# Expert stage of a two-layer gated block: new addresses for the tiles of normalized tokens and gated activations

## The reference

```python
x = x + tanh(g_xattn[0]) * L0_xattn(layernorm(x), ctx, ctx, ...)      # retention over four heads
x = x + tanh(g_ffn[0])   * L0_ffn(layernorm(x), w1, w2, gamma)        # ternary weights, 512 -> 2048 -> 512
x = x + tanh(g_xattn[1]) * L1_xattn(ctx, ctx, layernorm(x), ssm_kernel, D, 8)
x = x + tanh(g_ffn[1])   * L1_ffn(layernorm(x), Wg, bg, Wgate, ...)   # experts
```

```python
gate = xf @ Wg + bg                                  # 8 logits, the 6 highest are kept
w = softmax(kept)[:, :6] * routed_mask
g = einsum('td,ndh->tnh', xf, Wgate) + bgate
u = einsum('td,ndh->tnh', xf, Wup) + bup
eo = einsum('tnh,nhd->tnd', silu(g) * u, Wdown) + bdown
share = silu(xf @ Ws_up + bs_up) @ Ws_down + bs_down
out = einsum('tnd,tn->td', eo, w) + share
```

## Time and profile before

| what | value |
|---|---|
| median of three runs | 2049.53 us (2049.35 to 2049.96) |
| span of the profiled execution | 2045.1 us |
| outside the span, against that median | 4.4 us |
| PE busy | 1937.3 us, 95% |
| PEld busy | 1565.1 us, 77% |
| DVE busy | 1480.1 us, 72% |
| ACT, POOL busy | 1029.0 us, 1037.1 us |
| granted clock of TensorE, mean | 0.977 |

### The profile page before, as it was taken

The page is one execution under the profiler, slowest core; times in us unless marked ns, Lnnn a source line. Parts: engine busy times, 40 slices in busy tenths (PEclk is TensorE's granted clock), DMA queues, the critical chain, the costliest instruction groups (busy, mean ns, idle before and its releaser), DMA issues.

```text
span 2045.1 us, 27663 instructions
## 1 busy us (share of the span) xinstructions
PE 1937.3 (95%) x10020; PEld 1565.1 (77%) x10050; DVE 1480.1 (72%) x2229; ACT 1029.0 (50%) x1468; POOL 1037.1 (51%) x788
## 2 busy tenths in 40 slices
PE   6999779999996769999999999999999999999998
PEld 6888656666653658888888888888888888888786
DVE  6777579888884867867876876876886787687422
ACT  4457457767774354345336337336435633633532
POOL 1110154444430945765655665656566566666454
PEclk9999889999998879999999999999999999999999
DMA  6776325655664213324234233242242423422422
GB/s 221 291 247 241 150 62 142 165 163 139 140 131 116 73 31 124 106 70 139 76 105 145 78 114 129 77 120 97 95 124 68 140 80 100 148 75 72 133 90 67
DMA packets 170115, 249.72 MB, mean 122 GB/s; under 512 B 91356, under 2 KB 92764, under 8 KB 163708
## 3 DMA queue, kind: packets, MB, share of 16 engines
q1 hardware_dynamic: 169692, 247.86, 39.7%
q10 hardware_dynamic: 288, 0.10, 0.0%
HBM read 193.13 MB, written 33.69 MB: 111 GB/s over the span
## 4 chain that ended last, share of the span: by engine, by line
PE 64%; POOL 2%; issue 1%; DVE 1%; DVEq 0%; ACT 0%; POOLq 0%; ACTq 0%
PE e_ps_out L54 6%; PE e_ps_out L55 6%; PE e_ps_out L56 6%; PE e_ps_u L54 6%; PE e_ps_u L56 6%; PE e_ps_u L55 6%; PE e_ps_g L54 4%; PE e_ps_g L56 4%; PE e_ps_g L55 4%; PE e_ps_m L55 4%; PE e_ps_m L56 4%; PE e_ps_m L54 4%; PE e_ps_m L2873 1%; PE e_ps_m L2827 1%; PE e_ps_m L2863 1%
## 5 line engine op out<-in xcount | busy, mean ns | idle before, releaser
L1418 POOL TENSOR_TENSOR e_gu_lo<-e_gu_raw,e_gu_hi 128x1024 fp32r<-128x1024 f32 (+1 forms) x128 | 289.3, 2263 | 183.4 <-ACT e_gu_hi L1722 183.4
L2277 DVE TENSOR_REDUCE e_x3T<-e_zp 128x128 f32<-128x1024 f32 x124 | 258.4, 2084 | 6.5 <-ACT x_held L1837 5.3
L1423 POOL TENSOR_TENSOR e_dn_lo<-e_dn_raw,e_dn_hi 128x512 fp32r<-128x512 f32 x128 | 180.6, 1414 | 112.6 <-ACT e_dn_hi L1728 111.8
L54 PE MATMUL e_ps_u<-e_xn_hi,e_gu_hi 128*128 128x512 f32 x512 | 205.2, 401 | 0.0
L54 PE MATMUL e_ps_out<-e_hd_hi,e_dn_hi 128*128 128x512 f32 x512 | 204.0, 399 | 0.0
L56 PE MATMUL e_ps_u<-e_xn_hi,e_gu_lo 128*128 128x512 f32 x512 | 202.1, 395 | 0.0
L55 PE MATMUL e_ps_out<-e_hd_lo,e_dn_hi 128*128 128x512 f32 x512 | 202.0, 394 | 0.0
L55 PE MATMUL e_ps_u<-e_xn_lo,e_gu_hi 128*128 128x512 f32 x512 | 201.9, 394 | 0.0
L56 PE MATMUL e_ps_out<-e_hd_hi,e_dn_lo 128*128 128x512 f32 x512 | 201.9, 394 | 0.0
L2209 DVE TENSOR_TENSOR e_hd_lo<-gate_held,e_hd_hi 128x512 fp32r<-128x512 f32 x128 | 147.4, 1152 | 67.9 <-ACT e_hd_hi L1752 67.7
L1430 POOL TENSOR_TENSOR gate_held<-e_sg,e_wb 128x512 f32<-128x512 f32 x96 | 137.4, 1432 | 113.0 <-ACT e_sg L1736 71.7
(11 more groups left out here) (316 smaller groups left out, 5059.8 us busy)
## 6 DMA issues: line engine op xcount, KB each, us to landing
e_gu_raw<-in_mgu SPq DMA_DIRECT2D x96, 512.0 KB, 3.8
e_dn_raw<-in_md SPq DMA_DIRECT2D x128, 256.0 KB, 2.8
e_wb<-wts SPq DMA_DIRECT2D x8, 1536.0 KB, 7.4
c<-in_ctxT SPq DMA_DIRECT2D x8, 1024.0 KB, 7.0
raw_w<-in_w1T SPq DMA_DIRECT2D x8, 1024.0 KB, 5.0
x_held<-in_w2T SPq DMA_DIRECT2D x8, 1024.0 KB, 7.4
gates<-gate_held SPq DMA_DIRECT2D x8, 1024.0 KB, 5.5
vals<-o SPq DMA_DIRECT2D x8, 1024.0 KB, 5.2
```

The source lines that it names most:

```text
L54: nc.tensor.matmul(out, w_hi, x_hi, start=first, stop=False, skip_group_check=skip)
L1418: nc.gpsimd.tensor_tensor(gu_lo[:, s % 2, a], gu_raw[:, s % 2, a], f32(gu_hi[:, s % 2, a]), ALU.subtract).then_inc(gulo_done, 1)
L1423: nc.gpsimd.tensor_tensor(dn_lo[:, s % 2], dn_raw[:, s % 2], f32(dn_hi[:, s % 2]), ALU.subtract).then_inc(dnlo_done, 1)
L2277: nc.vector.tensor_reduce(x3T[:, lb].rearrange("p (b n) -> p b n", b=B)[:, :, hh * CD:(hh + 1) * CD], zv(5, (1, 8), (21, 8)), AX.X, ALU.ad ...
```

## The change

The tile `skip` is allocated behind all other tiles of the expert stage instead of in their middle. Two tiles that nothing writes or reads are added: `gap_xn`, 16 floats (64 bytes) in each partition, ahead of `xn_hi`, and `gap_hd`, 64 floats (256 bytes), ahead of `hd_hi`. No instruction changes but for its addresses.

```diff
     zp = sb("zp", [P, B, ZW])
-    skip = sb("skip", [P, NCH * CHD])
     x3T = sb("x3T", [P, KT, CH])
 
     xnat = sb("xnat", [P, TJ, D])
+    gap_xn = sb("gap_xn", [P, 16])
     xn_hi, xn_lo = sb("xn_hi", [P, KT, CH], F32R), sb("xn_lo", [P, KT, CH], F32R)
     wb = sb("wb", [P, NE, CH])
     wT, wTf = sb("wT", [WROWS, CH], F32R), sb("wTf", [8, CH])
     sg, sgw, hd = sb("sg", [P, CH]), rest[:, 3], rest[:, 2]
     lgT = sgw[0:16]
+    gap_hd = sb("gap_hd", [P, 64])
     hd_hi, hd_lo = sb("hd_hi", [P, 2, CH], F32R), sb("hd_lo", [P, 2, CH], F32R)
...
     gb = sb("gb", [P, KT])
+    skip = sb("skip", [P, NCH * CHD])
```

## The result

The changed kernel takes 2037.51 us (median of four runs, 2037.0 to 2038.83). The kernel before takes 2049.44 us beside it (four runs, 2048.5 to 2049.96). The ratio is 0.9945, with a 95% interval of 0.9931 to 0.9959: 11.9 us or 0.55% less. The forecast was 17.5 us less.

What follows compares the result with a forecast made beforehand. The expert stage was taken to be bound by back-to-back TensorE matmuls; 3180 settled steps gaining 5.5 ns each give 17.5 us, all else zero, for 2032 us. Likeliest range 2026 to 2038 us, overall 2002 to 2053.

Steps and rivals of the forecast that it cites:

- The 5.5 ns: Long matmuls: 232.3 ns a step in the expert stage against 226.8 early, laid to distance between streamed operand and loaded weights.
- the rival that something else in the stage sets the pace: Expert stage: weights' route or PSUM sharing causes the 5.5 ns, distance is innocent; no change, 2049.5 us; chance 0.16.
- That 256 bytes are a repeat: Operand distances count modulo 256, read from a 288-column unit: 131.1 ns at 0 and 256, 133.3 at 128 and 384.
- I take the settled value, 226.8: Expert stage's long matmuls at distance 64: after unsettled starts, runs settle at 226.8 ns a step instead of 232.3.
- the only lasting lock in the rows is the low one: Reason for 226.8: unsettled runs average 230 to 233 ns at distance 0 or 128; the only lasting lock lies below.
- 3180 x 5.5 = 17.5 us: Expert stage: 3180 of 4224 long matmuls settle and gain 232.3 - 226.8 ns each, 17.5 us in all.
- Unsettled starts: The first four to nine steps, say six, of each of 174 long-matmul runs keep their old pace.
- halfway between that of 0 and that of 128: Long matmuls at a pace midway between distances 0 and 128: 4224 x 2.75 = 11.6 us gained, 2038 us.
- The slower rival: Long matmuls at 64 lock into slow steps: 0.2% slower from 233.3 ns on, 2065 us at 236; chance 0.16.
- The costs put at nothing: ScalarE, VectorE and GpSimd: shifted addresses cost zero, as do the load of `skip` and the transposes.
- two of the signs that the prediction named: Profile after: VectorE, ScalarE, GpSimd keep counts and means; PE stays at 200 of 200 us between 900 and 1850 us.

Runs made afterwards that it cites:

- 320 for 64: The changed kernel, tokens 64 and activations 320 bytes past a multiple of 512 from their weights: 2037.51 us; with both at 64, 2037.39 us.
- 256 for 0: Changed kernel without the 64-byte gap, so tokens at 0 and activations at 256 from their weights: 2029.22 us.
- At 32: Changed kernel with a 32-byte gap ahead of the tokens and none ahead of the activations, both 32 bytes past a multiple of 512 from their weights: 2052.33 us.
- 192: Changed kernel with a 192-byte gap ahead of the tokens and none ahead of the activations, both 192 past a multiple of 512 from their weights: 2053.26 us.
- 224: Changed kernel with a 224-byte gap ahead of the tokens and none ahead of the activations, both 224 past a multiple of 512 from their weights: 2052.92 us.

## Why the prediction was right, and where it was wrong

**What held.** The expert stage is bound by its matmuls one after another: of the 10.7 us that it became shorter, 10.5 lie in the long steps. The 5.5 ns between the earlier trace rows are the distance's: that was inferred from two stretches that differ in much else, and it is shown by moving one operand (226.6 ns) and by moving both (2049.82 us, no change). Hence the rival that something else in the stage sets the pace falls. The Trainium skill, "SBUF — State Buffer", "Who interferes with whom", tells of two independent read ports of TensorE that never wait; tails of 226.6 to 233.4 ns at a granted clock of 1.00, with only addresses between them, do not agree with it here. Through what the two operands meet is not shown. That 256 bytes are a repeat was read from one unit of nine steps a half; the kernels with 320 for 64 and 256 for 0 bear it out.

**What failed: "I take the settled value, 226.8".** The argument was that the only lasting lock in the rows is the low one, so a run at 64 either settles there or stays unsettled. There is a further lasting state: at 64 the steps repeat in threes with a mean of 228.8 ns from the first to the last of 95. The premise was also a misreading of the kernel before. Its tail is not unsettled: in the trace its steps repeat in sevens of about 231, 232, 228, 230, 232, 241 and 233 ns from the first to the last, a lasting state of its own that starts printed to 10 ns hide. The term "3180 x 5.5 = 17.5 us" is therefore mis-sized in its price. At the tail's pace all 4224 steps would gain 4224 x (232.3 - 228.8) = 14.8 us, and the starts of the runs take from that. Over all runs the mean step became 3.0 ns shorter, about 12 us on the 4224 - 174 = 4050 steps inside them. Measured are 11.9 by the medians and 10.7 in the profile from the stage's first matmul on.

**Unsettled starts.** The prediction took six steps of each run off and left them at their old price. Averaged over the 174 runs, the first four steps at 64 take 231 to 233 ns and the later ones 228 to 231, so fewer than six are lost. At 0 the first seven take 228 to 231 ns, and from the eleventh on it is 226.7: the count was about right, but these steps gain as well. With 226.7 the prediction's sum would be 3180 x 5.6 = 17.8 us for distance 0, and the kernel without gaps gains 20.0. So the form of the sum is near and some 2 us low even for the right distance; what failed is that it was given the pace of 0 for 64.

**The halfway price.** The upper end of the likeliest one's range, "halfway between that of 0 and that of 128" (2038), meets the time by accident. At 32 the pace is 233.4, not between 226.7 and 228.8, and at 192 and 224 the time is above that at 128: there is no slope between the points along which a halfway value could be taken. The slower rival, "from 233.3 ns on", is what 32, 192 and 224 do: 233.3 to 233.4 ns, 3 to 4 us over the kernel before. A gap of 32 bytes instead of 64 would have put the change on that side.

**The costs put at nothing.** ScalarE and GpSimd keep their counts and, within 2 us, their busy times. VectorE does not: two of the signs that the prediction named did not come out as it said. The means of `e_kv_lo` and `e_x3T` rose, and PE shows idle time in the middle, 0.87 us, with VectorE as the releaser. It is small beside 11.9 us. It does not come from the moved addresses: at 32, 192 and 224, with the same tiles moved, `e_kv_lo` takes 968 to 987 ns, and with the weights alone moved, at 226.6 ns a step, it takes 1038. So in these kernels it goes with PE's pace; through what is not shown.

**What stays open.** Why 0 and 64 have a low pace of their own and the other four distances none is not settled; nor is which weights count, those in use or those loaded meanwhile. Distances of 96 and 160 bytes and those that are not multiples of 32 were not tried, nor was a shift in the first stages, where all distances are multiples of 512.

## What to carry to other kernels

Where matmuls follow one another without idle time, read their price from the distance of the starts in the timeline: the group's mean duration moved by 2 ns at most here while the time fell by 0.55%. Look at where the streamed operand lies against its weights: here a small tile in the middle of the large ones cost 20 us, and with it last and no padding the kernel was as fast as any version tried. A pace between two measured points is not to be had by halving: measure the point, or keep to the one that is known.

## What the runs showed of the hardware that was not expected

- fp32r matmuls with 128x128 weights and 512 columns, back to back at a granted clock of 1.00, take 226.6 to 233.4 ns a step by the distance of their operands alone, and the low values found are 0 (226.7) and 64 (228.8) modulo 256, with 233.4 at 32 between them.
- The pace is a lasting pattern of a run, not a price of one instruction: threes of 226, 229 and 232 ns at 64; at 128 sevens with a mean of 232.3 in one kernel's tail and pairs of 237 and 229 in another's.
- Moving the low halves of the weights alone lengthens two of the three matmuls of a product (232.5 and 234.2 ns in the tail, against 226.7 for the first; one run).
- In the kernels whose tail goes at 226.6 to 228.8 ns `e_kv_lo` on VectorE takes 1031 to 1051 ns, in those at 232.3 to 233.4 ns 968 to 987, whether or not its own tiles were moved. In the changed kernel one wait of 0.87 us on PE is all that the profile shows of it in mid-stage.
